# Local attention in a hybrid network on one core: spans of 16 queries with 48 keys in place of 32 with 64, and where the last swap copies stand

## What is computed

```python
def _L2_attn_ref(x, Wq, Wk, Wv, Wu, bu):      # b=8, t=1024, e=64
    h, k = (8, 32)
    xp = jnp.pad(x, ((0, 0), (k - 1, 0), (0, 0)))
    q  = (x  @ Wq.T).reshape(b, t, h, e) / e ** 0.25
    kk = (xp @ Wk.T).reshape(b, t + k - 1, h, e) / e ** 0.25
    v  = (xp @ Wv.T).reshape(b, t + k - 1, h, e)
    idx = jnp.arange(t)[:, None] + jnp.arange(k)[None, :]
    dot = jnp.einsum('bthe,btkhe->bthk', q, kk[:, idx])
    attn = jax.nn.softmax(dot, axis=-1)
    out = jnp.einsum('bthk,btkhe->bthe', attn, v[:, idx]).reshape(b, t, h * e)
    return out @ Wu.T + bu
...
t = t + _L2_attn_ref(_ln_t(t), L2_attn_Wq, L2_attn_Wk, L2_attn_Wv, L2_attn_Wu, L2_attn_bu)
```

## Time and profile before

| | |
|---|---|
| median of 3 runs | 1521.3 us (1521.09 to 1521.32) |
| the profiled execution | 1520.63 us |
| its span in the trace | 1518.9 us |
| PE busy | 1362.2 us (90%), 10754 records |
| DVE, ACT, POOL busy | 629.4, 591.5, 176.7 us |
| mean granted clock of PE | 0.953 |
| attention block, first matmul to the next block's | 484.4 to 737.3 us |

### The profile page before, as it was taken

How to read it: one execution, slowest core, us unless ns; L and a number is a source line. 1 busy time by engine, 2 the same in 40 slices (tenths; PEclk the granted TensorE clock), 3 DMA queues, 4 the chain that set the end, 5 groups by cost and what they waited for, 6 DMA issues and landing times. The chain is left out here.

```text
span 1518.9 us, 27460 instructions
## 1 busy us (share of the span) xinstructions
PE 1362.2 (90%) x10754; PEld 871.6 (57%) x10754; DVE 629.4 (41%) x942; ACT 591.5 (39%) x1029; POOL 176.7 (12%) x175
## 2 busy tenths in 40 slices
PE   8999968889886899999699999999999999948767
PEld 5223357778775777777555555555555555536444
DVE  3981131121113677777532332333332323335662
ACT  3986742225674444444522222222222222223350
POOL 4000029400003222222100000000000000003000
PEclk9979979999998899999999999999999999979978
DMA  4900000000006000000000000000000000040001
GB/s 105 112 1 1 1 3 0 0 0 0 0 0 222 2 2 2 2 2 2 1 1 0 0 0 0 0 0 0 0 0 0 0 0 0 0 112 1 0 1 56
DMA packets 34302, 23.91 MB, mean 16 GB/s; under 512 B 24653, under 2 KB 28781, under 8 KB 34237
## 3 DMA queue, kind: packets, MB, share of 16 engines
q1 hardware_dynamic: 33853, 21.92, 6.6%
q10 hardware_dynamic: 384, 1.07, 0.3%
HBM read 20.80 MB, written 2.18 MB: 15 GB/s over the span
## 5 line engine op out<-in xcount | busy, mean ns | idle before, releaser
L1107 PE MATMUL sp_f<-hankel,sp_ut 128*128 x2304 | 420.9, 344 | 0.0
L1107 PEld LDWEIGHTS sp_f<-hankel,sp_ut 128*128 128x128 f16 x2304 | 222.8, 98 | 216.8 <-issue 27.6
L1146 ACT COPY sp_sums<-sp_f 64x1023 f32<-64x1023 f32 x128 | 129.0, 1008 | 428.5 <-PE sp_f L1107 428.5
L1169 DVE COPY sp_sums<-sp_f 64x1024 f32<-64x1024 f32 x128 | 155.3, 1213 | 91.8 <-PE sp_f L1107 91.8
L1167 DVE COPY sp_mix<-mix 128x512 f32 x64 | 27.4, 427 | 282.5 <-PE sp_f L1107 282.5
L1118 PE MATMUL sp_o<-sp_sums,sp_mix 128*64 128x128 f32 (+2 forms) x1024 | 123.7, 392 | 0.0
L502 PE MATMUL convv<-runningv,toeplitz 128*128 128x128 f32 x610 | 86.6, 289 | 15.0 <-DVE runningv L519 14.9
L502 PEld LDWEIGHTS convv<-runningv,toeplitz 128*128 128x128 f32 x610 | 75.0, 193 | 26.6 <-DVE runningv L519 26.6
L502 PE MATMUL convh<-runningh,toeplitz 128*128 128x128 f32 x610 | 84.3, 285 | 4.3 <-DVE runningh L519 1.2
L1118 PEld LDWEIGHTS sp_o<-sp_sums,sp_mix 128*64 128x64 f32 x1024 | 63.1, 134 | 37.5 <-issue 15.5
L801 POOL TENSOR_TENSOR win_probs<-win_probs,win_inv 128x1024 f32<-128x1024 f32 x32 | 60.8, 1901 | 186.5 <-DVE win_inv L969 186.5
(11 more groups left out here) (309 smaller groups left out, 1860.8 us busy)
## 6 DMA issues: line engine op xcount, KB each, us to landing
hankel<-phi_rows SPq DMA_DIRECT2D x32, 256.0 KB, 6.8
ex_w<-in_L_ffn_weight SPq DMA_DIRECT2D x1, 2080.0 KB
m_plus<-in_L_ffn_M_phi_plus SPq DMA_DIRECT2D x2, 1024.0 KB, 13.9
m_minus<-in_L_ffn_M_phi_minus SPq DMA_DIRECT2D x2, 1024.0 KB, 16.6
out<-x SPq DMA_DIRECT2D x8, 256.0 KB, 3.3
x<-in_x ACTq DMA_DIRECT2D x2, 512.0 KB, 8.0
x<-in_x SPq DMA_DIRECT2D x2, 512.0 KB, 9.2
ar<-in_L_ffn_M_u SPq DMA_DIRECT2D x2, 192.0 KB, 3.4
```

Of the source, the lines that this page charges most:

```text
L1107: mm = nc.tensor.matmul(f_ps[b][:, lo:(half + 1) * BANK], ut[:, hu, b, i, :, :].rearrange("p a c -> p (a c)"), m.hankel[:, hf, ds(j * 2 + ...
L1146: nc.scalar.copy(sums[n][HALF[1], b, 1:T], f_ps[b][HALF[1], 0:T - 1]).then_inc(f_act, 1)
L1169: nc.vector.tensor_copy(sums[n][HALF[0], b, :], f_ps[b][HALF[0], :]).then_inc(f_dve, 1)
```

## The change

A chunk of 128 queries is cut into 8 spans of 16 queries with 48 keys each, where it was 4 spans of 32 with 64.

- `scores`: 32 matmuls in place of 16; the weights are four heads of 16 queries (64 rows by 64 columns), the moving operand 48 keys. The four quadrants of PE come in turn. The mask is 384 columns for each bank, its weights 16 rows by 128 columns (`win_rows`).
- `shifted`, the maxima, exponentials, sums and the normalisation cover 16 groups of 48 columns, 768 elements in place of 1024. `probs` keeps 64 columns per group, of which 16 are set to zero once by POOL.
- `windows_turned`: four transposes of 112 tokens in place of two of 128; ACT copies 512 columns in place of 256.
- `attend`: 32 matmuls of 64 moving columns, 48 rows of weights, in place of 16 of 128 with 64 rows.
- DVE's turn: the maximum, then add(i-1), then the two subtractions; before, add(i-1) stood behind the subtractions.
- The swap copies of the last two units move out of the norm's block into the attention's, on POOL behind the first normalisation. scores(24) waits for them.
- The mask is built from one block of 16 rows in the weights' block.

The diff, cut to its core:

```diff
-NW = CHUNK // WINDOW
-KEYS = 2 * WINDOW
+SUB = 16
+NW = CHUNK // SUB
+KEYS = WINDOW + SUB
+EARLY = 6
...
+def swap_copies(nc, m, pool, units, done, ready=None):
...
+    for u in units:
+        if ready is not None:
+            pool.wait_ge(ready, u + 1)
+        some = slice(u * PER_UNIT, (u + 1) * PER_UNIT)
+        for p in range(2):
+            link(nc.gpsimd.tensor_copy(m.swapped[HALF[1 - p], some, WINDOW:PIECE], m.pieces[HALF[p], some, WINDOW:PIECE]))
+        if u % 2:
+            first = u // 2 * PER_PAIR
+            for t in (m.pieces, m.swapped):
+                link(nc.gpsimd.tensor_copy(t[:, first + 1:first + PER_PAIR, 0:WINDOW], t[:, first:first + PER_PAIR - 1, CHUNK:PIECE]))
...
+            m.swapped_early = swap_copies(nc, m, pool, range(EARLY), 0, out_ok)
...
+                nc.gpsimd.memset(probs[:, :, KEYS:C], 0.0).then_inc(padded, 1)
+                for i in range(CHUNKS):
+                    if i == 1:
+                        pool.wait_ge(n_ok, 1)
+                        swap_copies(nc, m, pool, range(EARLY, 2 * G), m.swapped_early)
                     pool.wait_ge(inv_ok, i + 1)
...
-                    for low in range(2):
-                        keys = m.pieces[:, i, low * WINDOW:low * WINDOW + 2 * KEYS]
-                        mm = nc.tensor.transpose(xt_ps[:, low, :], keys, m.ident[:, :])
+                    for t in range(4):
+                        mm = nc.tensor.transpose(xt_ps[0:LONG, t, :], m.pieces[:, i, t * SUB:t * SUB + LONG], m.ident[:, :])
...
                 def scores(i):
+                    if i == SECOND:
+                        pe.wait_ge(m.swap_ok, m.swapped_early + 6)
...
-                        nc.tensor.matmul(s_ps[:, r, :, :, :].rearrange("p i w n -> p (i w n)"), m.ident_bf[:, :], m.win_mask[:, :], start=True, stop=False)
+                        nc.tensor.matmul(s_ps[:, r, 0:NW * KEYS], m.win_rows[:, :], m.win_mask[:, :], start=True, stop=True)
                     for p in range(2):
-                        for w in range(NW):
-                            for r in range(2):
-                                keys = image(p, r)[HALF[r], i, w * WINDOW:w * WINDOW + KEYS]
-                                mm = nc.tensor.matmul(s_ps[:, r, p, place(w), :], queries[HALF[r], p, w, :, :].rearrange("p h n -> p (h n)"), keys,
+                        for jj in range(2):
+                            for high in range(2):
+                                for c in range(2):
+                                    for r in range(2):
+                                        j = 4 * high + 2 * jj + c
+                                        mm = nc.tensor.matmul(scored[HALF[c], r, 4 * p + 2 * jj + high, :], queries[HALF[r], p, j, :, :].rearrange("p h n -> p (h n)"),
+                                                              image(p, r)[HALF[r], i, j * SUB:j * SUB + KEYS], start=False, stop=True, skip_group_check=True)
...
                     for p in range(2):
-                        for low in range(2):
+                        for t in range(4):
                             for high in range(2):
+                                rows = slice(high * C, high * C + KEYS)
                                 for r in range(2):
-                                    mm = nc.tensor.matmul(z_ps[HALF[r], high, p, low, :, :].rearrange("p h n -> p (h n)"), xt[odd][HALF[high], low, p * C:(p + 1) * C],
-                                                          probs_t[HALF[high], p, r, low, :], start=True, stop=True)
+                                    mm = nc.tensor.matmul(z_ps[HALF[r], high, p, t, :, :].rearrange("p h n -> p (h n)"), xt[odd][rows, t, p * C:(p + 1) * C],
+                                                          probs_t[rows, r, p, t // 2, (t % 2) * C:(t % 2 + 1) * C], start=True, stop=True)
...
-                    nc.scalar.activation(probs[:, :, :, :, :].rearrange("p i r w n -> p r i (w n)"), shifted[:, :, :, :, :].rearrange("p r i w n -> p r i (w n)"), ACT.Exp).then_inc(p_ok, 1)
+                    nc.scalar.activation(probs[:, :, 0:KEYS], shifted[:, :, :], ACT.Exp).then_inc(p_ok, 1)
...
                 def body(i):
                     if loops(i, 1):
-                        shift(i + 1)
+                        largest(i + 1)
                     if loops(i, -1):
                         add(i - 1)
+                    if loops(i, 1):
+                        shift(i + 1)
                     take_probs(i)
```

More of the change, by code:

```diff
@@ L797, in _ @@
             def _(pool):
-                def normalise(i):
+                nc.gpsimd.memset(probs[:, :, KEYS:C], 0.0).then_inc(padded, 1)
[3 more added lines that the diff above has]
+                        swap_copies(nc, m, pool, range(EARLY, 2 * G), m.swapped_early)
                     pool.wait_ge(inv_ok, i + 1)
-                    whole = probs[:, :, :, :, :].rearrange("p i r w n -> p (i r w) n")
+                    whole = probs[:, :, 0:KEYS]
                     nc.gpsimd.tensor_tensor(whole, whole, rinv[:, :].to_broadcast([P, NT, KEYS]), ALU.mult).then_inc(n_ok, 1)
-                for i in range(CHUNKS):
-                    normalise(i)
             @block.tensor
@@ L815, in query @@
                         for p in range(2):
-                            mm = nc.tensor.matmul(q_ps[:, p, n, :], m.win_qk[HALF[p], n, :],
-                                                  m.pieces[HALF[p], i, WINDOW:PIECE], start=True, stop=True)
+                            mm = nc.tensor.matmul(q_ps[:, p, n, :], m.win_qk[HALF[p], n, :], m.pieces[HALF[p], i, WINDOW:PIECE], start=True, stop=True)
                     mm.then_inc(q_ok, 1)
@@ L848, in turn_probs @@
                         pe.wait_ge(pt_dve, i)
-                    for p in range(2):
-                        for r in range(2):
-                            for low in range(2):
-                                mm = nc.tensor.transpose(t_ps[:, p, r, low, :], probs[:, p, r, 2 * low:2 * low + 2, :].rearrange("p a n -> p (a n)"), m.ident[:, :])
+                    else:
+                        pe.wait_ge(padded, 1)
+                    for r in range(2):
+                        for p in range(2):
+                            for jj in range(2):
+                                v = 8 * r + 4 * p + 2 * jj
+                                mm = nc.tensor.transpose(t_ps[:, r, p, jj, :], probs[:, v:v + 2, :].rearrange("p a n -> p (a n)"), m.ident[:, :])
                     mm.then_inc(pt_ok, 1)
@@ L902, in take_queries @@
                         act.wait_ge(s_ok, i)
-                    nc.scalar.activation(queries[:, 0, :, :, :], q_ps[:, 0, :, :].rearrange("p h (w n) -> p w h n", w=NW), ACT.Copy).then_inc(q_act, 1)
+                    nc.scalar.activation(queries[:, 0, :, :, :], q_ps[:, 0, :, :].rearrange("p h (j n) -> p j h n", j=NW), ACT.Copy).then_inc(q_act, 1)
                 def take_windows(i, odd):
@@ L991, in _ @@
                 take_queries(0)
+                largest(0)
                 shift(0)
@@ L1658, in weights_stage @@
         wut = sb("win_wut", [C, HEADS, C])
-        mask = sb("win_mask", [P, KEYS])
+        mask = sb("win_mask", [SUB, KEYS])
         phi_n = sb("phi_n", [FILTERS, T])
@@ L1704, in _ @@
                 pool.wait_ge(mk, 4)
-                for q in range(P // WINDOW):
-                    rows = mask[q * WINDOW:(q + 1) * WINDOW, :]
-                    nc.gpsimd.affine_select(out=rows, in_=rows, compare_op=ALU.is_ge, fill=MASKED, base=-1,
-                                            pattern=[[1, KEYS]], channel_multiplier=-1).then_inc(mk, 1)
-                    pool.wait_ge(mk, 2 * q + 5)
-                    nc.gpsimd.affine_select(out=rows, in_=rows, compare_op=ALU.is_ge, fill=MASKED, base=WINDOW,
-                                            pattern=[[-1, KEYS]], channel_multiplier=1).then_inc(mk, 1)
-                    pool.wait_ge(mk, 2 * q + 6)
-                for n in range(BANK // KEYS):
+                nc.gpsimd.affine_select(out=mask[:, :], in_=mask[:, :], compare_op=ALU.is_ge, fill=MASKED, base=-1,
+                                        pattern=[[1, KEYS]], channel_multiplier=-1).then_inc(mk, 1)
+                pool.wait_ge(mk, 5)
+                nc.gpsimd.affine_select(out=mask[:, :], in_=mask[:, :], compare_op=ALU.is_ge, fill=MASKED, base=WINDOW,
+                                        pattern=[[-1, KEYS]], channel_multiplier=1).then_inc(mk, 1)
+                pool.wait_ge(mk, 6)
+                for n in range(NW):
                     nc.gpsimd.tensor_copy(m.win_mask[:, n * KEYS:(n + 1) * KEYS], mask[:, :])
+                    nc.gpsimd.tensor_copy(m.win_rows[:, n * SUB:(n + 1) * SUB], m.ident[0:SUB, 0:SUB])
             @block.tensor
```

82 lines of the change are left out of this document (38 added, 44 removed).

## The result

| | before | after |
|---|---|---|
| median (lowest to highest) | 1521.3 us (1521.09 to 1521.32, 3 runs) | 1482.9 us (1479.07 to 1483.98, 4 runs) |
| ratio, 95% interval | | 0.975 (0.973 to 0.977) |
| profiled execution, its span | 1520.63, 1518.9 us | 1479.07, 1477.3 us |
| PE busy, records | 1362.2 us, 10754 | 1340.9 us, 12866 |
| attention block, first matmul to the next block's | 484.4 to 737.3 us | 478.0 to 697.4 us |

The change is 38.4 us faster by the medians. A fourth run of the kernel before took 2987.3 us, about twice the others, and is left out of its median. The forecast was 1479, the range 1468 to 1505; the median is 3.9 above the forecast, and the profiled execution, at 1479.07, is the fastest of the four.

The account below looks back on a forecast made before the run. The prediction took the attention block's loop of PE and DVE as the bound. Steady turns -33.6, border -3.5, start -4.6 and end -0.9 sum to -42.6 from 1520.6, giving 1478.0, 1479 as median; range 1468 to 1505 us.

Parts of the forecast that it names:

- 29 turns: Steady attention loop: the period falls from 7.38 to 6.22 us, -1.16 each turn, -33.6 us in all.
- The mechanism: Attention block: PE and DVE wait for each other each turn, one loop; both sides shrink, PE's 0.55 us wait becomes 0.04.
- 0.058 for four quadrants: Scores and attend: four small tiles on four quadrants take 0.058 us, so each step takes 1.10 us.
- turned keys: Key transposes on PE: two more at about 0.11 us each, +0.22, from 0.27 to 0.49 us.
- PE's own list: PE's output, turned probabilities and queries beside DVE's part of the turn: together 3.07 us.
- The start: Block's start: two half-clock waits through scores and mask -1.8 each, shorter DVE passes and exponentials -1.0; together -4.6 us.
- The border: Between norm and attention blocks: POOL's last swap copies move behind the first normalisation, hidden there; -3.5 us.
- The end: Block's last turn, waiting for inverse and normalisation: DVE -0.27, POOL -0.47, ACT -0.24; together -0.9 us.
- Rival 1: PE starts small tiles one by one whatever their quadrant: scores and attend 2.03 us each, total 1537 us; chance 0.11.
- Rival 2: 48-column groups cost DVE what 64 did, its part stays 3.62 us, period 6.73, total 1495 us; chance 0.05.
- Rival 3: Four quadrants at once but at 0.080 us a group: scores and attend 1.45 each, total 1501 us; chance 0.11.

Follow-up runs that it names:

- a_warm2: Kernel after plus 27 identity matmuls nobody reads, laid into PE's waits at the block's border and start, second measurement: 1479.6 us, ratio 0.9731.
- a_mask2: Kernel after with the mask and its weights held twice, so the two mask matmuls use different rows of PE: 1479.2 us, ratio 0.9738.
- after_third: The kernel after without any edit, measured a third time: 1481.6 us, ratio 0.9749 to the kernel before.
- a_order: Kernel after with DVE's old order, both subtractions ahead of the addition: 1478.9 us, ratio 0.9744 to the kernel before.
- a_scores2: Kernel after with the same 32 score matmuls reordered so neighbours use two of PE's four quadrants: 1501.9 us, ratio 0.9888 to the kernel before.

## Why the prediction was right, and where it was off

The profiled executions differ by 41.6 us in span, and the forecast summed -42.6; the medians differ by 38.4. Stage by stage, from the two traces (the start of the norm's block at 462.82 and 458.55 is POOL's first memset there):

| stretch | forecast | measured | how |
|---|---|---|---|
| ahead of the norm's copies, code not touched | 0 | -2.9 | 469.63 to 466.69 |
| border, first copy to query(0) | -3.5 | -3.5 | 14.80 to 11.26 |
| query(0) to output(0), start | -4.6 | -5.9 | 25.30 to 19.36 |
| 29 turns | -33.6 | -28.1 | 214.26 to 186.20 |
| last output step of the loop to the next block | -0.9 | +0.6 | 13.31 to 13.88 |
| behind the block, code not touched | 0 | -1.7 | 781.6 to 779.9 |

The total came out near for a reason that the forecast can't claim: 4.6 us of it lie in code that the change doesn't touch, but for the mask's setup, and behind that POOL waits 14.3 us before and 15.9 after. They are the spread from run to run; the start of the norm's block stands at 457.5 to 461.1 us in the ten traces of the experiments and at 462.8 in the profiled execution of before. What the change itself does is -37.0 in these two traces, and some -38.5 by the repeated medians, not -42.6.

**The mechanism was right.** The loop of PE and DVE, S to S, is what set the block, both sides of it shrank, and PE's wait in each turn is gone. Scores 1.08 (forecast 1.10), attend 1.10 (1.10), mask 0.43 (0.42), maximum to next start 1.01 (0.99), the subtractions 0.93 to the next start (0.94), addition 0.27 (0.26), copy 0.68 as before. Taking 0.058 for four quadrants, from a single tile and from a pair of column halves, was the step that decided the sign, and it held.

**The first term that was off: turned keys, 0.49 forecast, 0.58 measured.** I added 0.11 for each of two more transposes to 0.27. Four transposes take 0.58 (591.16 to 591.74): 0.155 for each of the two added. The row that I took the 0.11 from is of eight transposes with 128 rows out; why four with 112 are slower each was not tried. **PE's own list** was 3.13, where I had 3.07: the queries take 1.09, not "about 1.02". DVE at 3.02 was in turn better than my 3.11, as the addition waited for nothing in an undisturbed turn. Together the period is 6.31 to 6.32 in place of 6.22, which is 29 x 0.094 = 2.7 us of the missing 5.5.

**The second, which was not there at all: the pauses.** About 3 us in the trace, most of the rest. I had counted busy time only and never asked whether PE can be fed at half again the number of matmuls per turn in less time. The profile before had a row for the question, the packets of the instruction queue in part 3 of the page, first before and then after:

```profile
q8 instruction: 48, 0.79, 0.2%
```

```profile
q8 instruction: 65, 1.06, 0.3%
```

**The start** was better than forecast by 1.3. The two waits through mask and scores at half clock fell from 4.41 and 4.55 to 2.61 each, -1.8 and -1.9, as forecast. What I missed is a seam in the count: turn 0, with scores(2) in it, stood between the part that I called the start and the 29 turns, and I counted its own gain in neither. From the turned probabilities of chunk 0 to output(0) it is 7.31 before and 6.24 after, -1.07.

**The border** was right to 0.1 us, in the change and alone.

**The end** was off by 1.5. Of the last steps POOL's and DVE's savings are there (PE no longer waits for POOL in its last turn of probabilities), but output(29) holds a pause of 0.5, and the last output step ran at half clock. PE in the timeline of the kernel after:

```profile
683.51 1.57 PE L876 MATMUL z_ps<-win_heads_t,win_vo 128*64 128x128 f32 x16
...
694.69 1.98 PE L876 MATMUL z_ps<-win_heads_t,win_vo 128*64 128x128 f32 x16 [1.11 <-ACT win_heads_t L944]
```

Before it took 1.09. The mean granted clock is 0.68 from 694.0 to 695.5 and 0.50 from 695.5 to 697.0, so it fell about 694.5, ahead of this step. Whether it falls ahead of the block's end differs between executions: from the last output to the next block it is 1.82 us in a_warm2 and 1.81 in a_mask2, as before (1.82), but 2.69 in after_third and 2.70 in a_order, as here. A term of 0.9 can't foresee that.

**The rivals.** Rival 1 is refuted by a_scores2: the same records take 1.81 or 1.08 by their order alone. It had one thing right, and by luck: with two quadrants in use a record costs 0.028, as in its 0.029. The Trainium skill (TensorEngine Tiling (Array Packing), Instruction Overhead) gives each matmul about 60 cycles however few columns it moves; at 2.4 GHz that is an estimated 0.025 us. Measured, four records start in 0.057, 0.014 each, so the figure can't be a cost of each record, as the prediction took it. Per float32 matmul, which is two records, it is 0.028, a little above the figure; but the same 32 matmuls took 1.81 us in a_scores2, so no price per matmul sets the time either. On one quadrant a record starts every 0.057, longer than the figure. The measurement decides in each. Rival 2 fell with the rows of DVE above: its times follow the columns, with groups of 48 too. Rival 3, 0.080 for four, fell with the same 0.057.

## What to carry to other kernels

When the trace has a loop of two engines, add its two sides up separately and name which is late next; here that gave each step of the new period within 0.1 us, and said rightly that the two sides would end level. Small tiles on all four quadrants go at the pace of one if neighbouring matmuls use different quadrants, and the order of the loops alone is worth 40% of such a step. When a change multiplies PE's instructions, look at the instruction packets of the profile and at matmuls per microsecond beside the busy time, for a saving beyond the rate at which pauses set in may be handed back in them; here that lay between 13.3 and 14.9 matmuls per us.

## What the runs showed of the hardware

- Four records of float32 on the four quadrants, 64x64 with 48 moving columns, start in 0.057 us; with only two quadrants in turn, two do in the same time (a_scores2).
- Two bf16 matmuls with 16 rows of weights and 384 moving columns take 0.43 us to the next step's start on the same rows of PE and 0.27 on different ones (a_mask2).
- At 14.9 matmuls per us PE paused 2.5 to 4.1 us in 183, at 15.3 to 16.0 between 6.4 and 7.0, at 13.3 hardly at all (0.2), each time in the middle of a step and for 0.1 to 1.3 us.
- The pauses stand at fixed places of PE's code, whole multiples of about 126 weight loads apart, which is as often as packets of instructions come.
- 27 matmuls that nobody reads kept the granted clock at 1.00 where it was 0.50 for 14 to 17 us, and gave back about 3 us in the block; a part of it is lost again to the delay of the first query, and what is left is below what the times can tell.
